# One block of attention, Mamba and experts: forward convolution by halves, gate projections set between time-step projections, all gates opened together

## What is computed

```python
x = x + L0_conv(group_norm(x))         # attention, softmax over each row's 102 largest scores
t = tokens(x)
t = t + mamba_block(layer_norm(t))     # two directions, 256 inner channels, 16 states
t = t + moe(layer_norm(t))             # 8 experts, 2 per token

def _mamba(x, ...):                    # once per direction
    xs, z = split(x @ in_proj_w.T)     # 256 channels each
    xs = silu(conv4(xs) + conv_b)      # 4 taps along the tokens
    dbc = xs @ x_proj_w.T              # 16 rows for dt, 16 for B, 16 for C
    dt = softplus(dbc[:16] @ dt_proj_w.T + dt_proj_b)
    h[t] = exp(dt * A) * h[t-1] + dt * B * xs      # for each of 16 states
    y = sum_s(h * C) + xs * D
    return (y * silu(z)) @ out_proj_w.T
```

## Time and profile before

| | |
|---|---|
| runs (3), median | 1493.72 us |
| profiled execution, its own time | 1495.54 us |
| its span | 1493.7 us |
| mean granted TensorE clock | 0.937 of full |
| busy: TensorE, VectorE, ScalarE, GpSimd | 1262.7, 1200.8, 898.4, 836.4 us |

### The profile page before, as it was taken

How to read it: one execution, slowest core, us unless ns; L and a number is a source line. 1 busy time by engine, 2 the same in 40 slices (tenths; PEclk the granted TensorE clock), 3 DMA queues, 4 the chain that set the end, 5 groups by cost and what they waited for, 6 DMA issues and landing times. The chain is left out here.

```text
span 1493.7 us, 17449 instructions
## 1 busy us (share of the span) xinstructions
PE 1262.7 (85%) x4573; PEld 641.1 (43%) x4573; DVE 1200.8 (80%) x1388; ACT 898.4 (60%) x1247; POOL 836.4 (56%) x450
## 2 busy tenths in 40 slices
PE   3609888898998988988888989889898998888868
PEld 1307344344546434433444634434354733434343
DVE  2695799998796689999688679999779479999920
ACT  1626766766555766767464676676574676676612
POOL 3022388788152378778235258878517238878815
PEclk8859899999989889999999979999999988999979
DMA  2000112222030112222021012222103011322203
GB/s 77 14 0 2 46 71 84 85 92 77 16 113 15 31 57 86 85 86 97 17 77 66 4 58 79 91 85 86 56 1 114 16 37 65 98 85 84 85 1 127
DMA packets 30506, 92.00 MB, mean 62 GB/s; under 512 B 4790, under 2 KB 8764, under 8 KB 30428
## 3 DMA queue, kind: packets, MB, share of 16 engines
q1 hardware_dynamic: 30428, 91.10, 18.0%
HBM read 88.34 MB, written 2.75 MB: 61 GB/s over the span
## 5 line engine op out<-in xcount | busy, mean ns | idle before, releaser
L664 POOL TENSOR_TENSOR work<-expo,ring 128x1024 f32<-128x1024 f32 x128 | 300.1, 2365 | 164.4 <-DVE expo L1364 162.3
L664 POOL TENSOR_TENSOR ring<-ring 128x1024 f32<-128x1024 f32 x128 | 300.2, 2367 | 26.7 <-DVE ring L1364 26.7
L1364 DVE TENSOR_TENSOR_SCAN ring<-ring,ps 128x1024 f32<-128x1024 f32 x128 | 284.7, 2263 | 6.9 <-PE ps L1786 6.9
L1364 DVE TENSOR_TENSOR_SCAN expo<-ring,ps 128x1024 f32<-128x1024 f32 x128 | 285.6, 2270 | 0.0
L1822 PE MATMUL ps<-ring,ident 128*128 128x512 f32 x512 | 260.4, 615 | 25.5 <-POOL ring L664 18.7
L1822 PE MATMUL ps<-work,ident 128*128 128x512 f32 x512 | 241.1, 593 | 0.0
L953 ACT ACTIVATE ring<-dt_f,decay 128x1024 f32<-128x1024 f32 x128 | 147.0, 1148 | 118.9 <-DVE expo L1364 80.7
L719 ACT ACTIVATE b_dtx_tok<-dtx_tok,b_tok 128x256 f32<-128x256 f32 x448 | 189.2, 493 | 0.0
L1786 PE MATMUL ps<-ident,b_dtx_tok 128*128 128x128 f32 x896 | 121.8, 279 | 43.9 <-DVE expo L1364 40.1
L1786 PEld LDWEIGHTS ps<-ident,b_dtx_tok 128*128 128x128 f32 x896 | 96.8, 141 | 134.0 <-issue 69.2
L1822 PEld LDWEIGHTS ps<-ring,ident 128*128 128x128 f32 x512 | 83.7, 189 | 159.7 <-POOL ring L664 116.6
(11 more groups left out here) (280 smaller groups left out, 2075.6 us busy)
## 6 DMA issues: line engine op xcount, KB each, us to landing
ring<-c_rows SPq DMA_DIRECT2D x128, 512.0 KB, 3.6
b_dtx_tok<-comb_rows SPq DMA_DIRECT2D x16, 512.0 KB, 4.0
dtx_tok<-comb_rows SPq DMA_DIRECT2D x16, 512.0 KB, 4.7
x_c<-in_x SPq DMA_DIRECT2D x4, 512.0 KB, 3.3
out<-xs_f SPq DMA_DIRECT2D x4, 512.0 KB, 2.6
w<-in_L_ffn_w SPq DMA_DIRECT2D x2, 512.0 KB
ring<-in_L_attn_f_in_proj_w SPq DMA_DIRECT2D x1, 256.0 KB
ring<-in_L_attn_b_in_proj_w SPq DMA_DIRECT2D x1, 256.0 KB
```

The source lines that it names most:

```text
L664: pool.tensor_tensor(hc[odd][:, k, :], hs[odd][:, k, :], c_all[:, odd, :], ALU.mult).then_inc(hc_ready, 1)
L1364: v.tensor_tensor_scan(hs[odd][:, k, order], dA[:, k, order], dbu[:, order], 0.0, ALU.mult, ALU.add).then_inc(scan_ready, 1)
```

## The change

The forward block 1 is convolved by halves of 512 columns: `conv_tap_half` and `convolve_forward` stand for `conv_tap` and `convolve`, and the first half starts after the first half of the projection. The gate projection (0, 0) is cut in two and laid around the first time-step projection; B's transposes come behind four of the gate projections' halves and no longer ahead of the time steps, and those of the backward direction move to `backward_states`. The three PSUM tables are given anew. `z_gate` is gone: all four gates are copied, and opened with four silus in `open_gates`. The core of the diff (functions that only take a new argument or count are left out):

```diff
@@ -344,14 +344,15 @@
-        z_ps = ((ps45, ps01), (ps45, ps45))
-        tok_ps = ((ps01, ps01), (ps01, ps45))
-        b_tok_ps = (ps01, ps45)
+        z_ps = ((ps45, ps01), (ps45, ps67))
+        tok_ps = ((ps01, ps45), (ps01, ps45))
+        b_tok_ps = (ps45, ps01)
+        z_place = ((1, 2), (4, 3))
         dbc_ps = (ps23, ps45)
         dt_ps = ((ps67, ps23), (ps01, ps45))
-        conv_place = ((3, 1), (2, 4))
+        conv_place = ((4, 2), (3, 5))
         state_in = (ps23, ps67)
         score_ps = (ps67, ps23)
...
+            conv_tap_half(b, 0)
+def conv_tap_half(b, half):
+    act.wait_ge(conv_filled, 5 * b + 1 + half)
+    nc.scalar.activation(halves(conv_half[0][:, 1, :])[half], halves(conv_ps[0][1])[half], ACT.Identity,
+                         bias=conv_b[:, 0, 1:2],
...
@@ -889,7 +895,7 @@
-    for d, k in ((0, 1), (1, 0), (1, 1)):
+    for d, k in ((0, 0), (0, 1), (1, 0), (1, 1)):
         nc.scalar.activation(gate[:, d, k, :], gate[:, d, k, :], ACT.Silu).then_inc(gate_open, 1)
     nc.scalar.preload_act_table_set("natural_log_exp_and_others")
@@ -924,21 +930,22 @@
 def prepare(b):
-    conv_tap(b, 0, 1)
-    conv_tap(b, 1, 0)
+    conv_tap_half(b, 1)
+    conv_tap(b, 0)
     silu_of_sum(b)
     conv_silu(b, 0, 1)
-    conv_tap(b, 1, 1)
+    conv_tap(b, 1)
     conv_silu(b, 1, 0)
     b_and_c(b, 0)
     top_part(b, 0)
     conv_silu(b, 1, 1)
-    z_gate(b)
-    b_rows(b, 0)
     nc.scalar.preload_act_table_set("natural_log_exp_and_others")
     dt_log(b, 0, 0)
+    z_copy(b, 0, 0)
     dt_log(b, 0, 1)
+    z_copy(b, 1, 1)
+    b_rows(b, 0)
     z_copy(b, 0, 1)
 def direction(b, d):
@@ -966,7 +973,7 @@
     def to_tokens(k):
-        act.wait_ge(tok_filled, 6 * b + 2 + 3 * d + k)
+        act.wait_ge(tok_filled, 6 * b + 2 + 2 * d + k)
         act.wait_ge(turned_back, 2 * pairs)
         copy(dtx_tok[:, :, k * P:(k + 1) * P],
              tok_ps[d][k][:, :].rearrange("p (a c) -> p a c", c=P)).then_inc(tok_copied, 1)
@@ -976,13 +983,11 @@
         z_copy(b, 1, 0)
         decay_of(0, 1, first=True)
         to_tokens(0)
-        z_copy(b, 1, 1)
-        to_tokens(1)
         decay_of(1, 0)
-        decay_of(1, 1)
         b_and_c(b, 1)
         top_part(b, 1)
-        b_rows(b, 1)
+        decay_of(1, 1)
+        to_tokens(1)
         dt_log(b, 1, 0)
         middle_part(b)
         decay_of(2, 0)
...
+        b_rows(b, 1)
         decay_of(1, 1)
     with act.Fori(2 if d == 0 else 1, PAIRS) as r:
         decay_of(2 * r, 0)
...
+def convolve_forward(b, part):
+    dve.wait_ge(tap_ready, 4 * b + 1 + part)
+    for n in range(1, TAPS):
+        steps = 9 * b + 3 * part + n - 1
         if n > 1:
+            dve.wait_ge(conv_step, steps)
+        first = part * BANK + (n if part == 0 else 0)
+        to, src = slice(first, (part + 1) * BANK), slice(first - n, (part + 1) * BANK - n)
+        v.scalar_tensor_tensor(conv_half[0][:, 1, to], conv_ps[0][1][:, src],
+                               conv_w[:, 0, 1, TAPS - 1 - n:TAPS - n], conv_half[0][:, 1, to], ALU.mult,
...
@@ -1377,10 +1394,7 @@
 def apply_gate(b, d, k):
     g = (b * DIRS + d) * BLOCKS + k
     dve.wait_ge(y_ready, g + 1)
-    if d or k:
-        dve.wait_ge(gate_open, 3 * b + 2 * d + k)
-    else:
-        dve.wait_ge(z_copied, 4 * b + 1)
+    dve.wait_ge(gate_open, g + 1)
     v.tensor_tensor(gate[:, d, k, :], gate[:, d, k, :], ps[2 * k][:, :], ALU.mult).then_inc(gated, 1)
 def state_pair(b, d, r, turn):
@@ -1397,17 +1411,19 @@
     state_pair(b, d, PAIRS - 1, d)
 def mamba(b, following):
-    convolve(b, 0, 1)
+    convolve_forward(b, 0)
     if following is not None:
         group_coefficients(following)
-    convolve(b, 1, 0)
-    convolve(b, 1, 1)
+    convolve_forward(b, 1)
+    convolve_backward(b, 0)
+    convolve_backward(b, 1)
     cap_step(b, 0, 0)
     cap_step(b, 0, 1)
     time_step(b, 0, 0)
     dtx_forward(b, 0)
     time_step(b, 0, 1)
     dtx_forward(b, 1)
+    dve.wait_ge(z_copied, 4 * b + 2)
     products(b, 0, 0, 0, 0, first=True)
     scan_product(b, 0, 0, 0, 0, 0, 0, first=True)
     scan_product(b, 0, 0, 0, 0, 0, 1, first=True)
@@ -1716,19 +1732,20 @@
     sum_taps(1, range(TAPS), signal=True)
     project_x(1, 1, range(HALVES))
-def project_z(b, d, k):
+def project_z(b, d, k, parts=range(HALVES)):
     if (d, k) == (0, 0):
         pe.wait_ge(conv_summed, 3 * b + 2)
     elif (d, k) == (0, 1):
+        pe.wait_ge(conv_summed, 3 * b + 3)
+    elif (d, k) == (1, 1):
+        pe.wait_ge(dt_ready, b * DIRS * BLOCKS + 1)
+    else:
         pe.wait_ge(tok_copied, 6 * b + 1)
-    elif (d, k) == (1, 0):
-        pe.wait_ge(z_copied, 4 * b + 1)
-    else:
-        pe.wait_ge(z_copied, 4 * b + 3)
-    for h in range(HALVES):
+    for h in parts:
         last = mm(halves(z_ps[d][k])[h], z_in_t[:, d, k, :], halves(mx)[h], start=True, stop=True)
-    last.then_inc(z_filled, 1)
+    if HALVES - 1 in parts:
+        last.then_inc(z_filled, 1)
 def project_dbc(b, d, k):
@@ -1750,11 +1767,11 @@
         if d == 0:
             pe.wait_ge(conv_summed, 3 * b + 1)
         else:
-            pe.wait_ge(tok_copied, 6 * b + 3)
+            pe.wait_ge(tok_copied, 6 * b + 2)
     elif d == 0:
         pe.wait_ge(hi_ready, 2 * e + 2)
     else:
-        pe.wait_ge(tok_copied, 6 * b + 4)
+        pe.wait_ge(tok_copied, 6 * b + 3)
     rows = slice(PARTS * BC, PARTS * BC + DT_RANK)
     for h in range(HALVES):
         last = mm(halves(dt_ps[d][k])[h], dtproj_t[rows, d, k, :], dbc[d][rows, h * BANK:(h + 1) * BANK],
@@ -1788,11 +1805,7 @@
 def b_rows(b, d):
-    if d == 0:
-        pe.wait_ge(hi_ready, 2 * b * DIRS + 1)
-        pe.wait_ge(conv_summed, 3 * b + 3)
-    else:
-        pe.wait_ge(hi_ready, 2 * (b * DIRS + 2))
+    pe.wait_ge(*((z_copied, 4 * b + 1) if d == 0 else (tok_copied, 6 * b + 4)))
     passed(pe)
     for i in range(TILES):
         last = tr(b_tok_ps[d][:, i * D_STATE:(i + 1) * D_STATE], dbc[d][0:D_STATE, i * P:(i + 1) * P],
@@ -1805,9 +1818,9 @@
     if d == 1:
         pe.wait_ge(gated, b * DIRS * BLOCKS + k + 1)
     elif k == 0:
-        pe.wait_ge(z_copied, 4 * b + 2)
+        pe.wait_ge(z_copied, 4 * b + 3)
     else:
-        pe.wait_ge(tok_copied, 6 * b + 2)
+        pe.wait_ge(hi_ready, 2 * (b * DIRS + 2))
     for i in range(TILES):
         last = tr(tok_ps[d][k][:, i * P:(i + 1) * P], dtx[d][k][:, i * P:(i + 1) * P], ident[:, :])
     last.then_inc(tok_filled, 1)
@@ -1844,9 +1857,11 @@
     spread(b, 1, 1, 0)
     for k in range(BLOCKS):
         dtx_to_tokens(b, 1, k)
-    for k in range(BLOCKS):
-        pe.wait_ge(tok_copied, 6 * b + 5 + k)
-        skip_term(1, k)
+    b_rows(b, 1)
+    pe.wait_ge(tok_copied, 6 * b + 5)
+    skip_term(1, 1)
+    pe.wait_ge(tok_copied, 6 * b + 6)
+    skip_term(1, 0)
     add(b, 1, 0, 0, [0])
     spread(b, 1, 2, 1)
     add(b, 1, 0, 0, [1])
@@ -1864,28 +1879,28 @@
 def mamba(b, following):
     project_dbc(b, 0, 0)
     project_dbc(b, 0, 1)
-    project_z(b, 0, 0)
-    b_rows(b, 0)
+    project_z(b, 0, 0, [0])
     project_dt(b, 0, 0)
+    project_z(b, 0, 0, [1])
     project_dt(b, 0, 1)
     project_z(b, 0, 1)
-    project_z(b, 1, 0)
-    dtx_to_tokens(b, 0, 0)
+    project_z(b, 1, 1)
+    b_rows(b, 0)
     pe.wait_ge(parts_ready, b * DIRS + 1)
     pe.wait_ge(dt_ready, b * DIRS * BLOCKS + 2)
     spread(b, 0, 0, 0, first=True)
-    project_z(b, 1, 1)
+    project_z(b, 1, 0)
+    dtx_to_tokens(b, 0, 0)
+    project_dbc(b, 1, 0)
+    project_dbc(b, 1, 1)
+    spread(b, 0, 1, 1)
+    project_dt(b, 1, 0)
     dtx_to_tokens(b, 0, 1)
-    project_dbc(b, 1, 0)
-    spread(b, 0, 1, 1)
-    project_dbc(b, 1, 1)
-    project_dt(b, 1, 0)
-    b_rows(b, 1)
     project_dt(b, 1, 1)
+    spread(b, 0, 2, 0)
     pe.wait_ge(dt_ready, b * DIRS * BLOCKS + 3)
     skip_term(0, 0)
-    spread(b, 0, 2, 0)
     add(b, 0, 0, 0, [0])
     pe.wait_ge(dt_ready, b * DIRS * BLOCKS + 4)
```

More of the change, by code:

```diff
@@ L910, in b_rows @@
             def b_rows(b, d):
-                act.wait_ge(tok_filled, 6 * b + 1 + 3 * d)
+                act.wait_ge(tok_filled, 6 * b + (1, 6)[d])
                 copy(b_tok[:, d, :, :].rearrange("p a s -> p (a s)"),
@@ L1302, in norm_coefficients, with convolve_backward @@
                                        ALU.mult).then_inc(tu_coef, 1)
-            def convolve(b, d, k, taps=range(1, TAPS)):
-                g = 3 * b + 2 * d + k - 1
-                dve.wait_ge(tap_ready, g + 1)
-                half = conv_half[d]
-                for n in taps:
-                    if n > 1:
-                        dve.wait_ge(conv_step, (TAPS - 2) * g + n - 1)
+            def convolve_forward(b, part):
+                dve.wait_ge(tap_ready, 4 * b + 1 + part)
+                for n in range(1, TAPS):
+                    steps = 9 * b + 3 * part + n - 1
+                    if n > 1:
+                        dve.wait_ge(conv_step, steps)
[3 more added lines that the diff above has]
```

(13 more changed lines are left out.)

21 lines of the change are left out of this document (10 added, 11 removed).

## The result

The changed kernel took 1498.98 us (median of 18 executions, 1494.13 to 1500.83), the kernel before 1493.15 beside it (18 executions). The ratio is 1.0039, 95% interval 1.0026 to 1.0052: slower by 0.39%, 5.8 us. Forecast were 1487, so 6 us were to be gained and 6 were lost; the time lies within 1% of no change and inside the range given, but on the wrong side.

What follows compares the result with a forecast made beforehand. VectorE, fed by all other engines between attention and the states, was taken as the bound. Forward −3.1 and backward start +1.4, times four, gave −6.8: 1495.54 to 1488.7, then 1487 after a 1.8 median correction; range 1470 to 1502.

Steps and rivals of the forecast that it cites:

- Halves: Forward convolution in 512-column halves, 0.75 us each: last convolution ends 0.7 us earlier, none of it on the path.
- Time steps before B's transposes: Forward time-step product starts once `dbc` is copied: cap 2.0 us earlier, first products of states 2.8 us earlier.
- Backward time steps: Both backward `dbc` products stand together, 10.2 us of waits go, next products start at 187.2: gain 6.4 us.
- First turned product: First scan of a turned product starts at 194.5 for 202.12: gain 7.6 us per image at full clock.
- The clock takes part of it back: TensorE's clock drops in the forward direction cost +1.5, +2.0 and +1.0 us, leaving −3.1 per image; bounds 0 and 7.3.
- first fall: TensorE's clock drop at the forward time-step products: 0 to 3.1 us on the path, taken as +1.5.
- second fall: Clock drop around the backward time steps: +2.0 us before the turned scan, +1.0 for coming ahead of the second product.
- Backward start: Start of the backward direction: 0.4 us paid, plus an even chance of a 2.0 us clock loss, +1.4 per image.
- fourth rival: TensorE's new gap before the backward skip terms drops the clock in each image: +16 us, 1510; chance 0.10.
- third rival: Forward gain swallowed, both clock drops at the worst place, 7.3 of 7.6 us given back: 1493 to 1494; chance 0.16.
- third products wait there for more than 2 us: Sign that the forecast is wrong: clock drops in the backward start and VectorE's third products wait over 2 us.
- second rival: Only the forward time-step clock drop vanishes, with TensorE's idle gap: −5.1 us per image, −20 in all, 1473; chance 0.22.

Runs made afterwards that it cites:

- e10: Changed kernel with time-step products over all 128 rows and one dummy matmul behind B's backward transposes, second run of that version: 1470.27 us, 0.9866 of before.
- e7: Changed kernel with full-row time-step products and the dummy matmul, first half convolution waiting for the whole tap: 1465.94 us, 0.9823 of before.
- e4: Changed kernel with time-step products reading all 128 rows instead of 16, the added weights zero: 1476.15 us, 0.9894 of before.
- e5: Kernel before the change with time-step products reading all 128 rows instead of 16: 1480.19 us, 0.9939 of before.
- e8: Changed kernel with full-row time-step products in the forward direction only, 16 rows in the backward direction: 1486.64 us, 0.9966 of before.
- e1: Changed kernel with one 512-column dummy matmul behind B's backward transposes, ahead of the skip terms: 1495.62 us, 1.0023 of before.

## Why the prediction was wrong

The full-clock half of it was right to about a microsecond. e10 is the changed order at 2.4 GHz throughout, with its first image to compare:

- *Halves.* 2.32 / 3 = 0.77 each, 0.75 forecast. "None on the path": e7 shows it for the early start.
- *Time steps before B's transposes.* First cap 17.8 after `tu_bias` for 19.75: 1.9, forecast 2.0. First products forecast at 168.4 (26.9 after `tu_bias`), found at 27.6 where the clock holds.
- *Backward time steps.* Next products forecast at 187.2 (45.7), in e10 at 46.6.
- *First turned product.* Forecast at 194.5 (53.0), in e10 at 54.05: a gain of 6.6 in this image for the 7.6 of the text. Over four images it is 61.4 less 54.1 = 7.3.

But this gain is for the most part not the order's. It sets the new order at full clock against the old one with its falls. At full clock on both sides the order is worth 2.5 (the fourth images of e4 and e5), so by this one pair about 5 of the 7.3 were the clock's from the start, and they come only if the clock holds. The prediction counted them as gained by the order and gave back 4.5.

**The step that failed is "The clock takes part of it back": +1.5, +2.0 and +1.0, together 4.5 per image of 7.6.** It measured 61.0 less 54.1, 6.9: 2.6 for the first fall (for +1.5) and 4.3 for the second, which came ahead of the second product (for +2.0 and +1.0). The bounds stood at 0 to 7.3, and the truth was near their upper end. Three misjudgements made it so. First, the first fall was priced by the *present* wait of 1.50 ahead of the products; in images 2 to 4 it fell on the second forward time step itself, and the second cap waited 4.20 in the second image. Secondly, the second fall was priced by half of the 3.9 us that the clock needed to return once the work was dense. But VectorE waited for TensorE twice behind it, 2.69 and 3.18 in the first image. In e8, which has this fall alone, it slowed the second product, the spread, the skip term and the sum by 5.2 in the first image, and the turned scan came 4.9 later than in e10: nearly the whole of it was paid. Thirdly, the trace of before was misread: it says that the clock falls after the backward time-step products, and that a fall ahead of the second one would be new. It had been down from 182.7, and that product took 3.78 us, nearly twice its 1.98.

*Backward start.* The 0.4 at full clock measured 0.5 (e1). The fall was given 2.0 at even odds, +1.0; it cost 1.7 and came in every image: +1.7. So +2.2 for +1.4. The mechanism of the fourth rival was right here, with "the clock never fell there before" a poor argument against it, since the transposes and the idle ahead of the skip terms were new. That it came in all four images is partly chance: over the four traces that leave the gap it came in 13 of 16 images.

Together: 4 × (−0.5 + 2.2) = +6.8 for a forecast of −6.8; the four images' marks say +7.0, the medians +5.8. What came is the third rival's forward direction ("both falls come at the worst place") with most of the fourth's backward start. Their chances were given one by one; that both can come together, and that the two falls forward rest on one cause, the 16-row products, was not considered.

By the test that the text set ("third products wait there for more than 2 us") the forecast is wrong: 2.21. Of the other marks the tap's wait (2.7 an image, 2.8 forecast), the first caps and the turned products' wait (2.5, "2 to 4") were right, the time-step waits (28.7, "below 12") and the spread's (14.9, "under 4") wrong. With the clock held both come out (10.9 and 2.2 in e10).

The rule of the Trainium skill, page "TensorE: Matmul & The Clock Gate", section "HAM oscillation — how this bites in real kernels", which lays falls of the clock on idle gaps of the engine, stands as follows. It speaks of longer gaps than any in these stretches, of which the longest is 2.99 us (e5); the prediction stretched it to a gap of 1.07. In the backward start the trace agrees in kind, though not in the length of the gap: filling the 1.23 us keeps the clock (e1). For the forward falls it does not: the gap of 1.07 in the first image shrank to 0.26 in the changed kernel and the first fall came all the same, in all four images, and both falls went when the products got their full rows, with the same gaps (e4, e8). The second rival, built on that rule, was wrong for that reason.

## What to carry to other kernels

Before a reorder is priced, look at what TensorE does where its clock falls, and split the gain into what the order gives at full clock on both sides and what a held clock gives. If it is busy with operands of few rows, give them all rows (zero weights cost nothing in time): here that one line was worth 9 us in the old order and some 22 in the new (by the ratios), where the reorder alone lost 6. When VectorE's slack is removed, the granted clock of the engine that feeds it becomes part of the path, so price a fall at all that it slows; and a stage moved to a place where an engine waits should be checked for the gap that it leaves, which one dummy matmul may fill.

The best version seen is the change with full rows and the dummy: 0.9867 and 0.9866 of before in its two runs, 0.9823 and 0.9843 if the first half convolution also waits for the whole tap.
